# The vector engine's steps cut at every dependence, and the pattern products ahead of the key products

## What is computed

```python
def _ln(x):
    mu = jnp.mean(x, axis=-1, keepdims=True)
    var = jnp.var(x, axis=-1, keepdims=True)
    return (x - mu) * jax.lax.rsqrt(var + EPS)

def _attend(q, k, v):
    attn = jax.nn.softmax(jnp.einsum('bhnd,bhsd->bhns', q, k) * SCALE, axis=-1)
    o = jnp.einsum('bhns,bhsd->bhnd', attn, v)
    return o.transpose(0, 2, 1, 3).reshape(B, N, D)

# layer 0 (layer 2 has the same form, layer 1 one cross attention)
xm = _ln(x) * (1.0 + sc_sa) + sh_sa
x = x + g_sa * (_attend(*split_heads(xm @ qkv_w + qkv_b)) @ sa_proj_w + sa_proj_b)
x = x + _attend(_ln(x) @ q_w + q_b, context @ kv_w + kv_b) @ ca_proj_w + ca_proj_b
xm = _ln(x) * (1.0 + sc_ff) + sh_ff
x = x + g_ff * (gelu(xm @ fc1_w + fc1_b) @ fc2_w + fc2_b)

# layer 3
weights = jax.nn.softmax(q @ k.T * H ** (-0.5), axis=-1)
combined = concat([nx, weights @ v, anchor])
router_probs = jax.nn.softmax(combined @ router_W + router_b, axis=-1)
routed = sum over 3 experts of router_probs * (silu(combined @ e_w1 + e_b1) @ e_w2 + e_b2)
x = x + sigmoid(silu(combined @ gate_w1 + gate_b1) @ gate_w2 + gate_b2) * (routed @ out_w + out_b)
```

## Time and profile before

| | before |
|---|---|
| median of 3 runs | 1776.84 us |
| the profiled execution, whole | 1773.16 us |
| its span, first to last instruction | 1770.7 us |
| PE busy, its weight loads busy | 1674.2 us (95%), 1413.4 us (80%) |
| DVE busy | 1554.2 us (88%) |
| ACT busy | 1470.1 us (83%) |
| POOL busy | 805.1 us (45%) |
| mean granted TensorE clock | 0.994 of full speed |

### The profile page before, as it was taken

One profiled execution on the slowest core, in us unless ns is written; L12 is line 12 of the kernel. 1 busy time (PEld: TensorE's weight loads), 2 busy tenths in 40 slices (PEclk: granted clock), 3 DMA queues, 4 the chain that ended last, 5 costly groups with the idle time before them and its releaser, 6 DMA issues.

```text
span 1770.7 us, 83583 instructions
## 1 busy us (share of the span) xinstructions
PE 1674.2 (95%) x35621; PEld 1413.4 (80%) x35621; DVE 1554.2 (88%) x3984; ACT 1470.1 (83%) x3587; POOL 805.1 (45%) x1721
## 2 busy tenths in 40 slices
PE   5987899999999999999999999999999999999998
PEld 4766778888878888888888888878888878877887
DVE  6887889989989999889989998989999998999865
ACT  3675789888988988898898988889898887777896
POOL 5333434545454444444444444435444544444342
PEclk9999999999999999999999999999999999999999
DMA  7000000001000000000000000000000000000000
GB/s 230 3 16 8 18 24 18 15 18 30 18 24 24 9 24 18 24 24 24 19 13 19 24 24 24 24 3 24 24 24 24 24 15 18 18 15 15 3 6 16
DMA packets 57823, 41.81 MB, mean 24 GB/s; under 512 B 13553, under 2 KB 56177, under 8 KB 57329
## 3 DMA queue, kind: packets, MB, share of 16 engines
q1 hardware_dynamic: 57456, 36.46, 7.1%
HBM read 31.99 MB, written 4.46 MB: 21 GB/s over the span
## 4 chain that ended last, share of the span: by engine, by line
PE 61%; DVE 23%; ACT 7%; issue 4%; POOL 2%; DMA 2%; SPq 1%; DVEq 0%; POOLq 0%
PE half L1028 8%; PE half L904 7%; PE half L930 7%; DVE top L1178 6%; PE half L945 6%; PE half L973 5%; PE half L963 4%; PE half L1037 4%; PE half L777 3%; PE half L891 3%; PE half L956 3%; PE half L880 3%; PE half L876 3%; DVE q_heads L1170 2%; PE half L926 2%
## 5 line engine op out<-in xcount | busy, mean ns | idle before, releaser
L1178 DVE TENSOR_REDUCE top<-half 128x32 f32<-128x2048 f32 x160 | 364.5, 2279 | 30.4 <-PE half L904 29.2
L1347 ACT ACTIVATE pT<-half 128x512 f32<-128x512 f32 x640 | 329.9, 604 | 59.4 <-PE half L930 57.5
L723 POOL TENSOR_TENSOR shifted<-moments,eps 128x2 f32<-128x2 f32 x256 | 50.4, 197 | 424.1 <-DVE moments L1144 421.7
L930 PE MATMUL half<-q_heads,k_heads 32*128 32x128 f32 x5120 | 232.2, 297 | 1.8 <-issue 1.8
L1382 ACT ACTIVATE pT<-half,mod 128x64 f32<-128x64 f32 x896 | 196.7, 338 | 22.1 <-PE half L1028 20.8
L930 PEld LDWEIGHTS half<-q_heads,k_heads 32*128 32x128 f32 x5120 | 201.4, 186 | 3.6 <-issue 2.2
L904 PE MATMUL half<-k_heads,q_heads 32*128 32x128 f32 x5120 | 190.1, 283 | 10.9 <-issue 5.2
L745 POOL TENSOR_TENSOR top<-top 128x32 f32<-128x32 f32 x160 | 39.9, 249 | 349.4 <-DVE top L1178 349.3
L725 POOL TENSOR_TENSOR rstd<-shifted,minus_halves 128x2 f32<-128x2 f32 x256 | 183.8, 718 | 20.1
L904 PEld LDWEIGHTS half<-k_heads,q_heads 32*128 32x128 f32 x5120 | 161.1, 187 | 37.8 <-issue 18.7
L945 PE MATMUL half<-pT,v_cols 128*32 128x64 f32 x10240 | 177.6, 220 | 13.4 <-issue 8.3
(11 more groups left out here) (154 smaller groups left out, 4018.2 us busy)
## 6 DMA issues: line engine op xcount, KB each, us to landing
gates<-gate_store SPq DMA_DIRECT2D x128, 128.0 KB, 3.1
x_rows<-x SPq DMA_DIRECT2D x32, 128.0 KB, 2.9
c_rows<-context SPq DMA_DIRECT2D x32, 128.0 KB, 2.2
out<-n_rows SPq DMA_DIRECT2D x32, 128.0 KB, 1.9
w_sb<-weights SPq DMA_DIRECT2D x1, 1856.0 KB, 7.2
w_sb<-weights SPq DMA_DIRECT2D x2, 512.0 KB, 6.0
logit_bias<-logit_store SPq DMA_DIRECT2D x64, 1.5 KB, 3.5
row_sb<-rows SPq DMA_DIRECT2D x1, 769.5 KB, 7.9
```

Source lines behind the costliest of these rows:

```text
L930: mm = nc.tensor.matmul(halves[HALF_OF[n]][:, g, tb * D:(tb + 1) * D], k_heads[s][part, tb, :, :], q_heads[s][part, tb, :, :], start=False ...
L1178: nc.vector.tensor_reduce(term[s][0], halves[HALF_OF[n]][:, :, :].rearrange("p g (c k) -> p g c k", k=SEQ), AX.X, ALU.max).then_inc(tops_r ...
L1347: nc.scalar.activation(turn_cols[s][:, g, :], halves[HALF_OF[n]][:, g, :], ACT.Exp, scale=ATT_SCALE).then_inc(scores_read, 1)
```

## The change

`GROUP_STEPS` now has 133 steps a group in place of 91. Each of the DVE pairs above is cut: the second instruction becomes a step of its own (moments, c_moments, shift, kvshift, inverse, weigh, back, add, l3_below, l3_total, l3_inverse, l3_top, l3_logits, l3_sum, l3_share, l3_add), so the digits of `SEQUENCE` can place steps of other streams between the two. `own_result` is gone; `makes(what, s, ins)` raises the semaphore and notes its count, and `after(what, s)` waits for that count at the head of the next step. In context the wait between the two L1131 goes. `SEQUENCE` is a new string of 4,274 characters (2,930 before); `HALVES` differs in one place. A bank that is now given back in a later step than it was taken (`frees()`) is counted where it is freed. The semaphore o_turned is split into one a stream. ACT's exponentials in layer 3 and POOL's work on the moments move with the steps that they follow.

In the scores step all 16 pattern products now come first, then all 16 key products; only the first pattern product of a bank carries the start flag and only the last key product the stop flag.

```diff
 def attention(a):
     return [("q", a), ("k", a), ("v", a), ("tops", None), ("lows", None), ("scores", None),
-            ("values", None), ("out", a)]
+            ("values", None), ("inverse", None), ("weigh", None), ("back", None), ("out", a)] + gated(a)
+
+def gated(layer):
+    return [("add", None)] if layer["gate"] is not None else []
+
+def moments(eps):
+    return [("stats", eps), ("moments", eps)]
+
+def columns(how):
+    return [("normal", None), ("cols", how)] + ([("shift", how)] if isinstance(how, tuple) else [])
...
 SEQUENCE = (
-    "f2102012200f0f20023f01012210f23014f2311430f42102f01031f02022f10022f30231f23310f40231f11043f00240f413"
...
+    "f210220011222000f00f220023f0101122110f233014f231144330000f421002222f0010331f0220222f11110022f302311f"
...
                             for g in range(TURNS):
                                 part = slice(32 * g, 32 * g + 32)
                                 nc.tensor.matmul(halves[HALF_OF[n]][:, g, tb * D:(tb + 1) * D], of_keys[part, 2 * tb:2 * tb + 2, :], low[s][part, :],
-                                                 start=True, stop=False)
+                                                 start=tb == 0, stop=False)
+                        for tb in range(GROUP):
                             for g in range(TURNS):
                                 part = slice(32 * g, 32 * g + 32)
                                 mm = nc.tensor.matmul(halves[HALF_OF[n]][:, g, tb * D:(tb + 1) * D], k_heads[s][part, tb, :, :], q_heads[s][part, tb, :, :],
-                                                      start=False, stop=True)
+                                                      start=False, stop=tb == GROUP - 1)
...
-                def own_result(ins):
-
-                    ins.then_inc(own, 1)
-                    count.next(own)
+                made, owned, held = {}, 0, {}
+
+                def makes(what, s, ins):
+
+                    nonlocal owned
+                    owned += 1
+                    ins.then_inc(own, 1)
+                    made[what, s] = own, owned
+
+                def after(what, s):
+                    dve.wait_ge(*made[what, s])
...
                     if kind == "values":
 
                         nc.vector.transpose(weighed[s], banks.take()[:, :]).then_inc(v_emptied, 1)
-                        dve.wait_ge(v_emptied, banks.uses)
-                        by_query = weighed[s].rearrange("p (n c) -> p n c", c=4 * HD)
-                        own_result(nc.vector.reciprocal(inv_sum[s][:, :, :], by_query[:, :, 2 * HD:WIDE]))
...
+                        made["by_query", s] = v_emptied, freed_by(n, FOR_VECTOR)
+
+                    if kind == "inverse":
+                        after("by_query", s)
+                        makes("inverse", s, nc.vector.reciprocal(inv_sum[s][:, :, :], by_query[s][:, :, 2 * HD:WIDE]))
```

More of the change, by code:

```diff
@@ L253, in bank_uses, with next_step, next_kv @@
     }.get(kind, (0, 0))
-USED = np.cumsum([bank_uses(kind, arg) for kind, arg, _ in ORDER], axis=0)
 FOR_VECTOR, FOR_SCALAR = range(2)
-def context_norms():
-    return {n: ORDER[[m for m in range(n + 1, len(ORDER)) if ORDER[m][2] == s][0]][1][0]
-            for n, (kind, _, s) in enumerate(ORDER)
-            if kind == "stats" and ORDER[[m for m in range(n + 1, len(ORDER)) if ORDER[m][2] == s][0]][0] == "kvnorm"}
-CONTEXT_NORMS = context_norms()
+def next_step(n):
+    return next(m for m in range(n + 1, len(ORDER)) if ORDER[m][2] == ORDER[n][2])
+def next_kv(n):
+    m = next_step(next_step(n))
+    return ORDER[m][1] if ORDER[m][0] == "kvnorm" else None
+CONTEXT_NORMS = {n: next_kv(n)[0] for n, (kind, _, _) in enumerate(ORDER) if kind == "stats" and next_kv(n)}
 FOLD_AT = {(kind, arg): n for n, (kind, arg, s) in enumerate(ORDER) if s is None}
@@ L282, with frees, freed_by @@
 assert max(FOLD_AT.values()) < first_scores(BY_SCORES[4])
-def next_step(n):
-    return next(m for m in range(n + 1, len(ORDER)) if ORDER[m][2] == ORDER[n][2])
 CONTEXT_NORMS_EACH = len(CONTEXT_NORMS) // GROUPS
-def used_by(n, ring, back=0):
+def frees():
+    fills, freed, pending, freed_at, by_step = [0, 0], [0, 0], {}, {}, []
+    for kind, arg, s in ORDER:
+        for side, uses in enumerate(bank_uses(kind, arg)):
+            for _ in range(uses):
+                fills[side] += 1
+                if side == FOR_VECTOR and kind in ("cols", "kvnorm", "l3_scores"):
+                    pending[s] = fills[side]
+                else:
+                    freed[side] += 1
+                    freed_at[side, fills[side]] = freed[side]
+        if kind in ("shift", "kvshift", "l3_below"):
+            freed[FOR_VECTOR] += 1
+            freed_at[FOR_VECTOR, pending.pop(s)] = freed[FOR_VECTOR]
+        by_step.append(tuple(freed))
+    return freed_at, by_step
+FREED_AT, FREED = frees()
+def freed_by(n, ring, back=0):
     s = ORDER[n][2]
@@ L521, in build @@
         c_moments_in, c_scaled = sem("c_moments_in"), [sem(f"c_scaled{s}") for s in range(STREAMS)]
-        o_turned = sem("o_turned")
+        o_turned = [sem(f"o_turned{s}") for s in range(STREAMS)]
         minus_in = [sem(f"minus_in{s}") for s in range(STREAMS)]
@@ L1130, in _ @@
                         for t in range(2):
-                            own_result(nc.vector.bn_stats(c_stats[s][:, t, :], c_rows[s][:, t, :]))
+                            m = nc.vector.bn_stats(c_stats[s][:, t, :], c_rows[s][:, t, :])
+                        makes("c_stats", s, m)
+                    if kind == "c_moments":
+                        after("c_stats", s)
                         for t in range(2):
@@ L1141, in _ @@
                             m = nc.vector.bn_stats(stats[s][:, t, :], x_rows[s][:, t, :])
-                        own_result(m)
+                        makes("stats", s, m)
+                    if kind == "moments":
+                        after("stats", s)
                         for t in range(2):
```

230 lines of the change are left out of this document (133 added, 97 removed).

## The result

| | before | after |
|---|---|---|
| median of 4 runs | 1775.71 us | 1754.31 us (1752.56 to 1763.35) |
| ratio of after to before | | 0.9906, 95% interval 0.988 to 0.9932 |
| span of the profiled execution | 1770.7 us | 1750.9 us |

The kernel became 0.9% faster, 17 us by the ratio and 21 by the medians. The direction was as forecast, but the forecast gain was 35 us, twice what came. The time lies inside the range of 1716 to 1773 us, though not in the part called the forecast (1720 to 1753, chance 0.56): it lies in the next one (1753 to 1772, chance 0.20), which stood for "only part 1 or little of it". So what has to be explained is a gain that is half missing.

A forecast was written before the change was run, and what follows sets the result against it. PE was taken as fullest, DVE and ACT close behind, no engine setting the time alone. 1773.16 - 16.6 (score steps) - 18.3 (DVE borders) = 1738.3, plus 3.7 to the median, gave 1742 us; range 1716 to 1773.

The forecast's parts named there:

- only part 1 or little of it: Outcome band of 1753 to 1772 us, where the score-step saving counts and the DVE saving brings little or nothing; chance 0.20.
- What bounds the kernel: Whole kernel: PE fullest, DVE and ACT close behind; work taken from PE or DVE worth about its part on the chain.
- Part 1: PE's score steps, pattern products first: 0.16 us less a step, 25.6 us of PE's work, 16.6 us of run time.
- Part 2: Borders between dependent DVE instructions, foreign work put between: 93 us less DVE time, 18.3 us of run time.
- signs of being wrong: Pattern groups 0.1 us or more apart; PE idle over 100 us with turned-back-attention waits; or DVE idle up as busy fell.
- What else moves: POOL, PSUM banks, PE's order and SP's transfers: shifts that cost nothing the prediction could find.
- DVE borders bring nothing: Rival: DVE's freed time becomes idle time before PE's products; 1760 us, or 1773 with dearer pattern groups; chance 0.20.
- The slower rival: Attention waits in DVE's line behind other streams' steps, each stream's way growing by 48 us: 1808 us; chance 0.10.
- a case of no change: Rival: both savings land in front of another wait, ACT at 88% busy in the middle; 1777 us, give or take 3.5; chance 0.06.

The follow-up runs named there:

- one table: Kernel before with Tanh for Gelu and Silu, so ACT loads tables twice, not 210 times: 0.9997; same edit with patterns first 0.9917, on the changed kernel 0.9847.
- the fifth kernel: Changed kernel in its order, with an added wait before each DVE step that follows a writer: 1.0254, 62 us above the changed kernel.

## Why the prediction was half right

**What bounds the kernel: right, and then used wrongly.** That several engines are near to each other was said, and that "no engine sets the time alone". The sum then took the chain's shares nearly at full value all the same: "work taken from PE or DVE is worth about the part of it that lies on the chain". This is the step under both terms that failed.

**Part 1, the step's cost: right.** 0.16 us a step were forecast, 0.15 came (1.33 to 1.18); 25.6 us of PE's busy time were forecast and 25.6 came in the changed kernel, at a slightly higher granted clock (0.996 against 0.994). The spacing of pattern groups that the trace of before could not show was 0.056 us, the end that I had taken. The Trainium skill (page "TensorE: Matmul & The Clock Gate", section "LDWEIGHTS (loading the stationary operand)") gives 107 ns for a load, not far from the 95 measured in bf16. It says nothing of how closely loads follow each other; the prediction's step from there to groups every 107 ns did not hold for these groups of four on different rows. The key products' busy time went from 232.2 us to 182.5, lower still than L904's 190.1.

**Part 1, what it is worth: too high.** The failed step is "104 x 0.16 = 16.6 us is my term". Measured alone it is 7 us. For longer score steps the number was good: 0.16 us more a step cost 18 us. A shorter one helps only as far as no other way is next. ACT was such a way: with ACT freed the same edit gave 14 us.

**Part 2, the size on DVE: right.** 66 us of busy time and 27 of idle time were forecast from 34 ns of gap and 84 ns of overlap; busy time fell by 63.6, and the idle time before the three dependent lines by 11.6 of 19.8. PE's share of the chain rose from 61% to 69%, as the forecast had asked of this part; with the borders alone it is 72%, with the patterns alone 58%. Of the signs of being wrong one came, PE idle by more than 100 us (102), but without the waits for the turned-back attention that were to go with it, and DVE's idle time rose by 44 us, two thirds of what its busy time lost. Waits added between independent instructions of the kernel before, with its order kept, cost 47 us. The Trainium skill's rule (page "VectorE: DVE Perf Modes", section "The DRAIN you can't avoid") has such waits cost nothing; these runs disagree with it. But that section adds that an instruction that is not held starts earlier, and the section "Two Vector instructions with no wait between them" has only a held one wait until every earlier one has finished. That fits the overlap of 84 ns; I had not weighed it in the forecast.

**Part 2, what it is worth: too high.** The failed step is "26% of 93 is 24.4 us. I take three quarters, 18.3 us". With the new order it is 9 us. The 26% was wrong in both directions: DVE time added cost 59% of its length in the old order and some 48% in the new one, DVE time taken away gave some 10% in either order (9 of 93 us, and 3 of 29 with an error of 4), or 14% with ACT freed. The kernel with 79 us more has 45% of its chain on DVE where there had been 23: what is added makes its own chain. A share of the chain was no price for DVE's time in this kernel.

**What else moves: partly wrong.** "PE's order keeps its sequence nearly everywhere" does not hold: of the 2,284 steps of PE compared, the longest order that the two lists have in common covers 1,591. What that reordering is worth by itself no run shows, since every kernel with the new order on PE also has parted borders or moved steps.

**The rivals.** "DVE borders bring nothing" gave 1760, from an overestimated part 1 and an underestimated part 2. The two together landed near the truth by luck: the patterns were worth 7 us and not 16.6, and the borders with their order 9 and not none. The slower rival did not come about in the changed kernel, and did so in the one with steps shifted without choice. What eats the gain, ACT just behind the chain, was not among the rivals as a mechanism of its own. The profile had it, at 1051 busy us of 1200, and the forecast named it only as a case of no change.

**What stays open.** About 10 of the missing 18 us went to ACT. What catches the rest, with one table still 27 us and not 35, was not tried, nor what the new order on PE costs or gives. Nor do the waits tell through which of ACT's steps it catches: PE's waits for ACT hardly differ between these kernels.

## What to carry to other kernels

In this kernel the chain of waits gave the price of work added to PE, and of nothing else: 26 us added there cost 18, but on DVE, with 26% of its time on the chain, 79 us added cost 47. Work taken away was worth far less than its share: score steps shorter by 24 us in all (160 of 0.15) gave 7, and 93 us of DVE time gave 9, with a new order. So before counting a saving, look for the engine whose busy share is next. Here ACT was 88% busy in the middle against PE's 97, ten points behind, and caught about 10 of the 35 us; the gain came out at half the sum. How near another engine must be to matter, one kernel doesn't show.

Cut a dependence only where the work put between is ready and the result has room: the same cut in badly chosen places made the kernel 150 us slower. And count in the trace what an edit did before reading its time: the waits that were to fall on 757 borders fell on 587 others too.

## What the runs showed of the hardware

- An independent DVE instruction starts 84 ns before the end of the one ahead (measured on the pairs of L1141 and of L1144), a dependent one 34 ns behind it. That was in the trace of before, but its weight was not expected: 672 waits between instructions that don't need each other made the kernel 2.6% slower. A second wait in front of an instruction whose first wait already covers it is not free either: the gap grew from 34 to 104 ns (605 gaps in the fifth kernel).
- Mixing bf16 and fp32 products in groups of four cost some 0.05 us at each change from bf16 to fp32. Sixteen and sixteen in place of four times four and four took the step from 1.33 to 1.18 us with the same products.
- Taking 208 table loads of 1.28 us from an engine that is 83% busy changed nothing (0.9997). With the patterns first, or with the whole change, the same loads were worth 0.4 and 0.6%.
- Part of the scatter from run to run goes with TensorE's clock. Of the eleven runs of the kernel before that stood beside the last kernels, the one of 1768.6 us had a mean granted clock of 0.996 and the one of 1783.6 us had 0.989, and the nine between had 0.991 to 0.995. The rows of single stretches show where it is lost: start:end, length, busy time by engine, granted clock, DMA share and GB/s in the first 240 us of the changed kernel, as the streams start:

```profile
0.00:60.00 60.00, 39.98 (x747) 32.50 (x748) 40.38 (x123) 27.77 (x62) 28.48 (x77) 0.94 0.55 171
60.00:120.00 60.00, 51.86 (x1208) 43.02 (x1206) 47.92 (x115) 39.92 (x88) 22.03 (x51) 0.94 0.06 12
120.00:180.00 60.00, 49.62 (x1182) 40.33 (x1176) 49.80 (x129) 41.30 (x89) 23.64 (x54) 1.00 0.03 8
180.00:240.00 60.00, 56.76 (x1292) 46.44 (x1296) 51.80 (x133) 52.34 (x123) 25.68 (x54) 1.00 0.05 14
```

  The kernel before has 0.94, 0.97, 0.94 and 1.00 there, and both have 1.00 from 240 to 1440 us. It means that some stretches of the start were granted the lower of the two levels (1.2 GHz in place of 2.4) for a part of their time. PE was idle for 20 and 8 of 60 us in the two at 0.94 here, but also for 10 in the third, at 1.00. The same shows at the other end: the kernel with steps shifted without choice, its PE idle for 111 of the 1200 us from 240 to 1440, had 0.97 there. No run here set out to change the clock.
